# Scan output through memory and a repeated read, in place of a diagonal tile and a spread on TensorE

## What is computed

```python
xh, gate = jnp.split(x @ W_in.T + b_in, 2, axis=-1)      # 512 channels each
xh = silu(conv4(xh) + conv_b)
x_ssm = xh @ W_ssm.T + b_ssm                             # 32 per position
def step(h, u):
    h = h @ A.T + u * Bv
    return (h, h @ Cv)                                   # one number s per position
s = scan(step, ...)
ssm_out = s[..., None] * xh + Dv * xh
y = (ssm_out * silu(gate)) @ W_out.T + b_out
```

## Time and profile before

| | us |
|---|---|
| median of 3 runs | 1017.08 |
| lowest and highest | 1014.64, 1022.38 |
| profiled execution | 1020.84 |
| its span, from first to last instruction | 1019.1 |

### The profile page before, as it was taken

One profiled execution on the slowest core, in us unless ns is written; L12 is line 12 of the kernel. 1 busy time (PEld: TensorE's weight loads), 2 busy tenths in 40 slices (PEclk: granted clock), 3 DMA queues, 4 the chain that ended last, 5 costly groups with the idle time before them and its releaser, 6 DMA issues. The chain is left out here.

```text
span 1019.1 us, 16854 instructions
## 1 busy us (share of the span) xinstructions
PE 863.1 (85%) x5964; PEld 663.5 (65%) x5964; DVE 597.7 (59%) x1441; ACT 405.0 (40%) x623; POOL 354.1 (35%) x290
## 2 busy tenths in 40 slices
PE   5998947789899888988989888887279999999993
PEld 4776725455666566655666556544279999999993
DVE  4889751545675777667676666643235555555542
ACT  4565611145444444445444454443043334233320
POOL 0333352222233434344342443223212442244422
PEclk9999967679998999999999998877579999999997
DMA  3117302444443445444344442400343222343100
GB/s 115 42 43 210 108 24 78 113 106 126 104 126 115 109 111 125 124 113 114 103 124 121 117 114 74 116 21 24 106 135 109 94 88 90 113 128 106 46 22 22
DMA packets 73432, 98.82 MB, mean 97 GB/s; under 512 B 10529, under 2 KB 60874, under 8 KB 73376
## 3 DMA queue, kind: packets, MB, share of 16 engines
q1 hardware_dynamic: 69920, 89.95, 32.0%
q0 software_dynamic: 3456, 8.13, 2.2%
HBM read 63.40 MB, written 35.73 MB: 97 GB/s over the span
## 5 line engine op out<-in xcount | busy, mean ns | idle before, releaser
L946 DVE TENSOR_REDUCE nmax<-ps_m 128x4 f32<-128x1024 f32 x128 | 156.6, 1224 | 174.6 <-PE ps_m L711 172.1
L903 ACT ACTIVATE pt<-ps_a 128x1024 f32<-128x1024 f32 x128 | 131.1, 1025 | 89.7 <-PE ps_a L721 88.3
L1216 ACT ACTIVATE hid<-ps_h 128x640 fp32r<-128x640 f32 x64 | 45.1, 705 | 151.3 <-PE ps_h L1156 151.3
L1156 PE MATMUL ps_h<-xt,w_hi 128*128 128x320 f32 x512 | 99.9, 318 | 1.0 <-DVE xt L1231 1.0
L1168 PE MATMUL ps_y<-w_hi,hid 128*128 128x256 f32 x640 | 85.3, 284 | 1.7 <-issue 1.7
L1265 DVE SCALAR_TENSOR_TENSOR hid<-ps_h,hid 128x640 fp32r<-128x640 f32 x64 | 52.7, 824 | 56.2 <-ACT hid L1216 55.7
L1156 PEld LDWEIGHTS ps_h<-xt,w_hi 128*128 128x128 f32 x512 | 80.0, 191 | 5.5 <-DVE hid L1265 3.9
L1168 PEld LDWEIGHTS ps_y<-w_hi,hid 128*128 128x128 f32 x640 | 80.1, 192 | 1.9 <-issue 1.9
L721 PE MATMUL ps_a<-qst,kst 49*128 49x256 f32 x512 | 67.8, 345 | 15.5 <-ACT pt L903 15.2
L721 PEld LDWEIGHTS ps_a<-qst,kst 49*128 49x128 f32 x512 | 40.8, 197 | 57.0 <-issue 31.8
L711 PE MATMUL ps_m<-kst,qst 48*128 48x256 f32 x512 | 66.9, 342 | 11.1 <-DVE nmax L946 5.9
(11 more groups left out here) (169 smaller groups left out, 1654.9 us busy)
## 6 DMA issues: line engine op xcount, KB each, us to landing
halves_dram<-half SPq DMA_DIRECT2D x64, 256.0 KB, 2.4
gated<-in_w SPq DMA_DIRECT2D x16, 1024.0 KB, 5.4
kst<-halves_dram SPq DMA_DIRECT2D x64, 128.0 KB, 3.1
qst<-halves_dram SPq DMA_DIRECT2D x64, 128.0 KB, 3.2
rows_dram<-blank SPq DMA_DIRECT2D x1, 5160.0 KB, 19.7
gated<-rows_dram SPq DMA_DIRECT2D x8, 645.0 KB, 4.2
x_raw<-in_x_t SPq DMA_DIRECT2D x8, 512.0 KB, 3.9
xres<-in_x SPq DMA_DIRECT2D x16, 256.0 KB, 3.6
```

The costliest lines, as they stand in the source:

```text
L903: nc.scalar.activation(pt[:, k % 4].rearrange("p s t q -> p (s t q)"), ps_a[:].rearrange("p s t q -> p (s t q)"), ACT.Exp).then_inc(s["exp ...
L946: nc.vector.tensor_reduce(nmax[:, q, :, :, h // 2].rearrange("p t s -> p s t"), ps_m[:], AX.X, ALU.max, negate=True).then_inc(s["max_done" ...
L1156: mm = pe.matmul(ps_h[:, f % 2, c2, 0:HC], w1[a][:, p, k, f * P:(f + 1) * P], xt[:, b, p, k, c2 * HC:(c2 + 1) * HC], start=(n == 0 and k = ...
L1216: nc.scalar.activation(hid[:, HI, f, :].rearrange("p (c n) -> p c n", c=2), ps_h[:, f % 2, :, 0:HC], ACT.Relu).then_inc(s["hid_hi"], 1)
```

## The change

In `mixer_in`, once `s_all` is made, TensorE transposes it, DVE copies the transpose into the tile `s_rows` (64 partitions, one for each cq and batch row, 128 wide), and SP stores it with four transfers into a tensor in memory, `scan`, of 16 rows x 256 positions. `s_all` now belongs to `mixer_in` alone. In `attend`, SP first waits for the four stores, and a new `load_s` reads one row of `scan` repeated over the 128 partitions into `sb`, which has two buffers; row n+2's is issued at the start of turn n, ahead of `load_x`. The diagonal tile, its mask (an input as well) and `spread_s` are gone. y is made in slot 11 instead of 13 and reads `sb`; `mixer_out` stands in slots 13 and 14 instead of 14 and 15, and takes over the two waits that `spread_s` had for `ps_d`.

```diff
@@ mixer_in, SP, after the store of the blank rows
+            sp.wait_ge(st_ready, 1)
+            for cq in range(4):
+                sp.dma_start(dram["scan"].rearrange("b (q c i) -> q b c i", q=4, c=4)[cq],
+                             c["s_rows"][B * cq:B * (cq + 1), :].rearrange("p (c n) -> p c n", c=4)[:, :, 0:L]
+                             ).then_inc(c["scan_out"], 16)
@@ mixer_in, PE, at the end
+            pe.wait_ge(s_ready, 1)
+            pe.wait_ge(gate_ready, MH * NG)
+            pe.wait_ge(c["loaded"], 16 * len(c["loads"]))
+            pe.transpose(ps_gate[0:4 * B, 0, 0:P], s_all[:].rearrange("p c b -> p (c b)"), c["eye"][:]
+                         ).then_inc(st_mm, 1)
@@ mixer_in, DVE, at the end
-            dve.wait_ge(s_ready, 1)
+            dve.wait_ge(st_mm, 1)
+            nc.vector.tensor_copy(c["s_rows"][:], ps_gate[0:4 * B, 0, 0:P]).then_inc(st_ready, 1)
+            dve.wait_ge(st_ready, 1)
@@ attend
-    diag = T("diag", [P, 4, 64], F32)
+    sb = T("sb", [P, 2, S], F32)
@@ attend, SP
+            def load_s(j, p):
+                settled(sp)
+                need(sp, s["y_done"], j - 1)
+                sp.dma_start(sb[:, p], dram["scan"][bass.ds(j, 1), :].to_broadcast([P, S])).then_inc(s_in[p], 16)
...
+            sp.wait_ge(c["scan_out"], 64)
+            load_s(0, 0)
             load_x(0, 0)
             load_ctx(0, 0)
 
             def step(n, p):
+                if on(n, -2):
+                    load_s(n + 2, p)
@@ attend, PE
-            def spread_s(j):
-                pe.wait_ge(s["diag_done"], j + 1)
-                need(pe, s["v_out"], j - 1)
-                need(pe, s["q_out"], j)
-                pe.matmul(ps_d[:, 0:S], ones[:], diag[:].rearrange("p c i -> p (c i)"), start=True, stop=True
-                          ).then_inc(s["sbc_mm"], 1)
...
             def mixer_out(j, t):
                 if t == 0:
                     pe.wait_ge(s["y_done"], j + 1)
+                    need(pe, s["v_out"], j - 1)
+                    need(pe, s["q_out"], j)
...
-                    if h == 12 and on(n, -1):
-                        spread_s(n + 1)
-                    if h in (14, 15) and on(n, -1):
-                        mixer_out(n + 1, h - 14)
+                    if h in (13, 14) and on(n, -1):
+                        mixer_out(n + 1, h - 13)
@@ attend, DVE
-                    if h == 7 and on(n, -1):
-                        need(dve, s["sbc_mm"], n + 1)
-                        nc.vector.tensor_tensor(diag[:], s_all[:, :, bass.ds(n + 1, 1)].to_broadcast([P, 4, 64]),
-                                                mask[:, None, :].to_broadcast([P, 4, 64]), ALU.mult
-                                                ).then_inc(s["diag_done"], 1)
-                    if h == 13 and on(n, -1):
-                        dve.wait_ge(s["sbc_mm"], n + 2)
+                    if h == 11 and on(n, -1):
+                        dve.wait_ge(s_in[q], use(n + 1, 16, q))
+                        need(dve, s["wout_mm"], n + 1)
                         for m in range(MH):
-                            op = nc.vector.scalar_tensor_tensor(y[:, m, :], ps_d[:, 0:S], c["d_col"][:, m:m + 1],
+                            op = nc.vector.scalar_tensor_tensor(y[:, m, :], sb[:, q], c["d_col"][:, m:m + 1],
                                                                 gated[:, m, bass.ds((n + 1) * S, S)], ALU.add, ALU.mult)
```

More of the change, by code:

```diff
@@ L63, in mixer_in @@
 def mixer_in(nc, T, PS, sem, c, dram):
-    gated, s_all = c["gated"], c["s"]
+    gated = c["gated"]
     HI, LO = 0, 1
@@ L93, in mixer_in @@
     ends = T("ends", [P, 4, B], F32)
+    s_all = T("s_all", [P, 4, B], F32)
     ps_xh = PS("ps_xh", [P, 4, 512], F32)
@@ L107, in mixer_in @@
     end_mm, ends_ready, s_mm, s_ready = sem("end_mm"), sem("ends_ready"), sem("s_mm"), sem("s_ready")
+    st_mm, st_ready = sem("st_mm"), sem("st_ready")
     LEVELS = 8
@@ L370, in _ @@
             nc.vector.tensor_copy(s_all[:], ps_xh[:, 0, 0:4 * B].rearrange("p (c b) -> p c b", b=B)).then_inc(s_ready, 1)
-            dve.wait_ge(s_ready, 1)
+            dve.wait_ge(st_mm, 1)
+            nc.vector.tensor_copy(c["s_rows"][:], ps_gate[0:4 * B, 0, 0:P]).then_inc(st_ready, 1)
+            dve.wait_ge(st_ready, 1)
             dve.wait_ge(gated_done, MH * NG)
 def attend(nc, T, PS, sem, c, dram):
-    gated, s_all = c["gated"], c["s"]
-    w, eye, ones, mask = c["w"], c["eye"], c["ones"], c["mask"]
+    gated = c["gated"]
+    w, eye, ones = c["w"], c["eye"], c["ones"]
     KT = S // P
@@ L439, in attend @@
     names = """setup_pool setup_dve setup_pe vo_row x_in0 x_in1 ctx_in0 ctx_in1 x_added
[L440 removed]
+        s_in0 s_in1 k_mm v_mm wout_mm x1t_mm q_mm mt_mm y_done k_out q_out k_hi q_hi k_split q_split v_out r1_done var1_ready
         rstd1 x1_done x1_kept x1t_out m_out k_stored q_stored k_in00 k_in01 k_in10 k_in11 q_in00 q_in01 q_in10 q_in11
@@ L447, in attend @@
     x_in, ctx_in = [s["x_in0"], s["x_in1"]], [s["ctx_in0"], s["ctx_in1"]]
+    s_in = [s["s_in0"], s["s_in1"]]
     k_in, q_in = ([[s[n + str(b) + str(lo)] for lo in range(2)] for b in range(2)] for n in ("k_in", "q_in"))
@@ L1353, in load @@
                 return tile
-            c["s"] = hold("s_all", [P, 4, B])
+            c["s_rows"] = hold("s_rows", [4 * B, P])
+            dram["scan"] = nc.dram_tensor("scan_dram", (B, S), F32, kind="Internal").ap()
             c["blank"] = hold("blank", [P, ROW])
@@ L1362, in decoder @@
             c["bv_rep"] = load("bv_rep", [P, KD, P], "(k p) n -> p k n", p=P)
-            for n, width in (("ones", P), ("mask", 64), ("tri", P), ("kinds", E), ("tokens", NT // P),
+            for n, width in (("ones", P), ("tri", P), ("kinds", E), ("tokens", NT // P),
                              ("b_out", D), ("b_o", D), ("d_col", MH), ("b_k", KD), ("b_q", KD)):
                 c[n] = load(n, [P, width])
-            for n in ("loaded", "blank_ready", "rows_blank"):
+            for n in ("loaded", "blank_ready", "rows_blank", "scan_out"):
                 c[n] = sem(n)
@@ L1435, in laid_out @@
     arrays["tokens"] = np.arange(NT, dtype=one).reshape(NT // P, P).T
[L1436 to L1439, removed]
     return {n: np.ascontiguousarray(v) for n, v in arrays.items()}
```

## The result

| | before | after |
|---|---|---|
| median, us | 1017.21 (4 runs) | 1029.08 (4 runs) |
| lowest and highest | 1014.64, 1022.38 | 1026.24, 1034.13 |
| profiled execution, its span | 1020.84, 1019.1 | 1028.48, 1026.6 |
| mean granted clock | 0.909 | 0.905 |

The ratio is 1.0116, with a 95% interval from 1.0059 to 1.0172: slower by 12 us, where the forecast was slower by 4.6.

A forecast was written before the change was run, and what follows sets the result against it. TensorE was taken to carry the turn, busy 27.66 to 29.35 us, with some 3 us of waits. 12 x 0.23 + 1.8 = 4.6 us on the median 1017.08 gave 1021.7 us, 0.45% more; range 1010 to 1029.

The forecast's parts named there:

- Longer clock: Rival, attention turns: all 12 take the shape of the longest, 12 x 0.81 = 9.7 us more, 1031.4 us; chance 0.09.
- two directions: Rivals on the clock, 12 turns: shorter, 10.6 us less, 1011.1 us; longer, 9.7 more, 1031.4 us; chance 0.09 each.
- DVE's list, +0.23 a turn: DVE's work between scores of slots 14 and 0: starts 1.81 us later, keys 0.23 us later; 12 turns, 2.8 us.
- y late: Rival, slot 11: y blocked more dearly, ends after 387.19, TensorE waits each turn; 0.5 us a turn, 1027.7 us; chance 0.14.
- y, taken at 0: Slot 11: y from SBUF meets POOL, takes 3.9 us instead of 1.66, still in time; cost 0, bound +0.5 a turn.
- The layout on rows 3: Slot 11: y's first part ends 383.72, others follow POOL's lines 577 and 579, the last two end by 387.2.
- by the rule: Slot 11: POOL's indirect DMA also holds y's first part, everything behind 0.3 us later, 12 x 0.3 = 3.6 us more.
- The spread, -0.12: Line 648 on TensorE, slot 12: removal saves 0.12 us a turn (2.52 against 2.40); the rest fills a wait.
- 11.6 / 16 = 0.73 us a turn: Rival, TensorE: the spread's full time comes off, 11.6 us less over 16 turns, 1005.5 us; chance 0.07.
- The boundary, +1.8: First block to attention block: transpose, copy and four stores start everything 2.5 us later; y ends about 154.85 against 153.07.
- one chain: After the boundary: mixer_out, r1, keys and all up to the wait at 180.19, so nothing gives the 1.8 us back.
- Hidden as told: Diagonal on DVE costed at nothing; stores and scan read, 4.8 us within 8.5; the loop's extra load, 0.45 us, hidden too.

The follow-up runs named there:

- old_slots: The changed kernel with y back in slot 13 and mixer_out in slots 14 and 15: 1017.54 us, ratio 1.0007 to the kernel before.
- pad_before: The kernel before with the spread's matmul issued twice in slot 12, same result written again: 1039.04 us, ratio 1.0168 to the kernel before.
- via_psum: The changed kernel, but DVE first copies sb into PSUM and y reads it there, still slot 11: 1022.6 us, ratio 1.0043 to the kernel before.

## Why the prediction was wrong

**The step that failed: the clock.** The sum priced work and waits and let the clock fall as before. "Longer clock" stood as a rival with 0.09 and 9.7 us. It is what happened: of +10.50 us in twelve turns, 6.9 lie behind the count, where only the clock differs. The rival's reason (every turn gets a small shift) was right, its chance was not. What should have raised it stood in the earlier trace rows: the same work took 30.96, 31.91 and 32.65 us, so the largest term by far in a turn was one that the sum held fixed. And it is not even in its two directions, which the prediction gave the same chance: without the extra matmuls, every kernel whose way to the keys grew had fewer full-clock turns than the three of before and a lower median clock, while `old_slots`, where it shrank, gained nothing. Why a small delay lowers the clock was not found; that it does, `pad_before` shows.

**DVE's list, +0.23 a turn.** The mechanism is there as told: no wait in front of the reduction of slot 0, and the keys later, by 3.59 / 12 = 0.30 us. But the 0.23 was made of a wrong part and lacked two. Half of `mixer_out` and the out-projection were counted at 1.93 + 1.06 = 2.99 us; in `via_psum` they took 455.30 - 452.51 = 2.79. So at full packing the list is level with before: 10.27 us, and its term is 0. In its place came the late y, 0.17 to 0.55 us in eight of the twelve turns (2.2 us in all), and DVE's 0.34 us at the loop's edge in three (1.1 with two smaller ones), which no row of before could show because the slack covered it. The turns of after are made of these two: 12.21 us to the keys with neither, 12.48 with y late, 12.54 with the edge of the loop, 12.83 with both.

**y, taken at 0.** The rival "y late" gave its own test: y ending 387.19 - 383.36 = 3.83 us after the turn of `onrm`. It ended at 416.46 + 4.18 - 416.60 = 4.04 in the turn shown, and later than 3.83 in eight of the twelve; at 3.71 to 3.76 in three in which POOL's first operation had started by the turn of `onrm`. The layout on rows 3 had the wrong parts held. It let the first part end unhindered and held the second and the third. In the trace the first two are held. Timeline of after, around the turn of `onrm` at 283.89, the first part of y by itself:

```profile
283.42 0.98 POOL L646 DMA_INDIRECT rows_dram<-pay,dest  x1 [0.30 <-issue]
283.75 2.25 DVE L1065 SCALAR_TENSOR_TENSOR y<-sb,d_col_sb,gated 128x256 f32<-128x256 f32 x1
284.41 1.30 POOL L603 TENSOR_TENSOR x2b<-xres,b_out_sb 128x512 f32<-128x512 f32 x1
285.79 1.34 POOL L605 TENSOR_TENSOR x2b<-x2b,xres 128x512 f32<-128x512 f32 x1
```

This part starts 0.66 us ahead of POOL's first operation, more than the 0.47 it takes alone, and ends at 286.00, 0.29 us behind that operation. What POOL was doing when it started is the indirect transfer; so it was that which already held it, and POOL's operation then went first. This is read from the times; no run takes the transfer away. A held part ended 0.28 to 0.29 us behind POOL's operation in eleven of the twelve turns, so the 0.3 us was right, and POOL's operations were hardly late (1.29 and 1.35 us in the turn shown, for 1.29 and 1.26). This is the case that the prediction worked out beside its sum, by the rule, with 3.6 us for twelve turns; it cost 2.2 of the way to the keys. The sum of the layout had a slip as well: 386.6 + 0.3 + 0.43 is 387.3, not 387.2, so that y was 0.1 us late by its own terms. The rival had 0.14. It came true together with that of the clock, and that they feed each other, a late y that then costs three times itself, was not in the text.

The Trainium skill (SBUF — State Buffer, Who interferes with whom) says that a DVE instruction with two SBUF inputs and a GpSimd instruction that reads SBUF lock each other out of a shared port. The trace agrees for POOL's two-input operations, 989 ns a part against 476 with one input moved to PSUM, and in the turn at 283.89 for its indirect transfer; that `diag` ran in its 0.43 us beside POOL's tensor_scalar is not explained by it.

**The spread, -0.12.** Confirmed: 2.39 us to the weighing, 30.84 against 30.96 for a turn at full clock, not the 11.6 / 16 = 0.73 us a turn for which line 648 is busy.

**The boundary, +1.8.** y's end is 1.5 us later, the memset 2.35 (2.5 told), the first scores 0.8. So 0.7 us did come back on the way that the text called one chain: the first sixteen records of `mixer_out` took 5.17 us for 5.90, at a granted clock of 0.71 for 0.62. Hidden as told: the diagonal on DVE, the four stores and the loads (they land in 1.5 and 3.7 us, 5.2 together where the estimate was 4.8 and 8.5 were free).

**In numbers.** 12 x 0.30 + 0.8 = 4.4 us for the work alone, beside 4.6 forecast; and 6.9 us for the clock. That the first two agree is luck: the 2.8 us of DVE's list were 0, y's 0 was 2.2, the loop's edge brought 1.1 that no term had, and of the boundary's 1.8 us 0.8 stayed.

## What to carry to other kernels

If neighbouring turns of the same work differ in granted clock, price a change by what it does to TensorE's pauses as well as by its length: here 0.3 us a turn became 1 us. A microsecond of matmuls that nobody needs, in a pause in front of the fall, gained 1.1% where the one shortening tried (`old_slots`) gained nothing that could be told. When an operation is moved to an earlier slot, follow what it passes on both of its queues: the spare time it fills there may hide overheads (here a loop's edge and a reduction that frees a buffer) that the trace of before does not show.

## What the runs showed of the hardware

- TensorE's clock fell in turns in which no pause was longer than 1.3 us (383.88 to 416.60: 1.30 for `hot`, 1.13 for `r1`, 0.95 for an exponential) and TensorE was busy for 28.5 of 32.7 us. The pauses for `hot` and the exponential are as long before the change, also in its full-clock turns; only that for `r1` grew, from 0.37. More turns fall when TensorE is delayed by 0.1 to 0.4 us a turn; by what rule stays open. The Trainium skill (TensorE: Matmul & The Clock Gate, HAM oscillation) tells of falls by long waits for transfers in each tile; no such wait is in these turns, and four matmul records, 1.13 us in all, in a pause of 1.3 us bought 11 us and raised the median granted clock from 0.913 to 0.935.
- A DVE operation with two SBUF inputs waits for POOL's two-input operation even when it is one of four queued back to back, and even when it started first, during an indirect transfer of POOL: parts of 474 ns took up to 2251, and ended 0.28 to 0.29 us behind POOL's operation. A copy of 0.43 us into PSUM in front of them took the hold away.
- DVE shows a pause of 0.33 to 0.38 us in front of its first work in a new pass of the loop (two turns a pass, three such edges) once nothing else hides it.
